# Attention by FFT products: two of four product sums made by accumulating DMAs, the constant's row put in ahead of them, correlation tiles handled in pairs

## What is computed

```python
qf = jnp.fft.fft(q, axis=2)
kf = jnp.fft.fft(k, axis=2)
corr = jnp.fft.ifft(qf * jnp.conj(kf), axis=2).real
topk = int(C * np.log(L))                       # 12
w, idx = jax.lax.top_k(corr.transpose(0, 1, 3, 2), topk)
w = jax.nn.softmax(w, axis=-1)
...
for i in range(topk):
    g = jnp.minimum(idx[:, :, None, :, i] + pos, L - 1)
    out = out + w[:, :, None, :, i] * jnp.take_along_axis(v, g, axis=2)
...
x = x + _L0_xattn_ref(_layernorm(x, axis=-1), ctx_4096, ctx_4096)
x = x + _L0_ffn_ref(_layernorm(x, axis=-1), A_w, B_w, Wq_w, keys)
```

## Time and profile before

| | |
|---|---|
| median of 3 runs | 2241.87 us (2239.7 to 2241.94) |
| profiled execution: span | 2240.4 us |
| PE, DVE, POOL, ACT busy | 97%, 76%, 70%, 55% of the span |
| a normal step, from one L578 to the next | 41.53 us |
| a normalizer step | 42.64 us |
| steps 3 to 30 | 22 normal, 6 normalizer |

### The profile page before, as it was taken

One profiled execution on the slowest core, in us unless ns is written; L12 is line 12 of the kernel. 1 busy time (PEld: TensorE's weight loads), 2 busy tenths in 40 slices (PEclk: granted clock), 3 DMA queues, 4 the chain that ended last, 5 costly groups with the idle time before them and its releaser, 6 DMA issues.

```text
span 2240.4 us, 30428 instructions
## 1 busy us (share of the span) xinstructions
PE 2170.8 (97%) x9664; PEld 1460.5 (65%) x9664; DVE 1712.2 (76%) x4081; ACT 1222.0 (55%) x2486; POOL 1570.1 (70%) x1023
## 2 busy tenths in 40 slices
PE   4899999999999999999999998899999999999999
PEld 2466565565565565565565564687888888787887
DVE  7999999999999999999999999744544444454443
ACT  4576676676676676676655535544434334443431
POOL 6899999999999999999999987433333333333420
PEclk9999999999999999999999999999999999999999
DMA  8132332332332332332321245544444444444431
GB/s 288 65 120 99 111 110 99 116 106 99 118 104 99 118 104 99 118 103 99 103 82 61 91 164 176 186 157 164 151 162 166 167 160 161 157 159 161 164 116 57
DMA packets 110420, 287.84 MB, mean 128 GB/s; under 512 B 7136, under 2 KB 7264, under 8 KB 109152
## 3 DMA queue, kind: packets, MB, share of 16 engines
q1 hardware_dynamic: 110304, 286.45, 37.1%
HBM read 219.32 MB, written 67.11 MB: 128 GB/s over the span
## 4 chain that ended last, share of the span: by engine, by line
PE 77%; DVE 11%; POOL 5%; issue 4%; ACT 2%; DMA 1%; SPq 0%; DVEq 0%; POOLq 0%; ACTq 0%
PE pair L691 7%; PE out L528 5%; PE out L530 5%; PE out L529 5%; PE z L528 5%; PE z L530 5%; PE z L529 5%; PE evac L602 4%; PE evac L603 4%; PE pair L528 4%; PE evac L578 4%; PE pair L530 4%; PE pair L529 4%; PE lag L642 4%; PE pair L591 4%
## 5 line engine op out<-in xcount | busy, mean ns | idle before, releaser
L1549 POOL TENSOR_TENSOR rows<-rows,cin 128x1024 f32<-128x1024 f32 x48 | 117.9, 2456 | 355.8 <-DMA rows<-out_dram 292.8
L691 PE MATMUL pair<-r_f,back 128*128 128x512 f32 x768 | 335.4, 593 | 0.0
L1495 POOL TENSOR_TENSOR r_f<-prod 128x1024 f32<-128x1024 f32 x128 | 306.0, 2402 | 24.0 <-DVE prod L931 22.1
L691 PEld LDWEIGHTS pair<-r_f,back 128*128 128x128 f32 x768 | 143.3, 190 | 167.8 <-issue 167.8
L528 PE MATMUL pair<-w_hi,wts_hi 128*128 128x512 f32 x512 | 206.5, 403 | 4.9 <-DVE w_lo L1049 2.9
L1244 ACT ACTIVATE xt_full<-tp 128x512 f32<-128x512 f32 x128 | 74.8, 584 | 245.4 <-PE tp L547 242.0
L528 PE MATMUL out<-b_hi,zt_hi 128*128 128x512 f32 x512 | 205.8, 402 | 1.5 <-ACT zt_hi L1433 1.5
L528 PE MATMUL z<-a_hi,xt 128*128 128x512 f32 x512 | 203.0, 397 | 1.9 <-DVE xt L888 1.9
L530 PE MATMUL pair<-w_hi,wts_lo 128*128 128x512 f32 x512 | 200.5, 392 | 0.0
L529 PE MATMUL pair<-w_lo,wts_hi 128*128 128x512 f32 x512 | 200.4, 391 | 0.0
L529 PE MATMUL z<-a_lo,xt 128*128 128x512 f32 x512 | 200.1, 391 | 0.0
(11 more groups left out here) (193 smaller groups left out, 5619.2 us busy)
## 6 DMA issues: line engine op xcount, KB each, us to landing
out_dram<-att_sb SPq DMA_DIRECT2D x32, 1024.0 KB, 4.3
rows<-out_dram SPq DMA_DIRECT2D x64, 512.0 KB, 3.6
cin<-out_dram SPq DMA_DIRECT2D x64, 512.0 KB, 4.0
xin<-in_x_dram SPq DMA_DIRECT2D x64, 512.0 KB, 3.7
out_dram<-rows SPq DMA_DIRECT2D x64, 512.0 KB, 2.6
vf<-in_ctx_dram SPq DMA_DIRECT2D x31, 1024.0 KB, 5.2
xf<-in_x_dram SPq DMA_DIRECT2D x30, 1024.0 KB, 5.1
stat_in<-in_x_dram SPq DMA_DIRECT2D x28, 1024.0 KB, 5.1
```

The costliest lines, as they stand in the source:

```text
L691: return nc.tensor.matmul(pair_ps[:, bank, :], back[:, 3 * bank + n, :], r_f[:, row, :], start=n == 0, stop=n == 2)
L1495: nc.gpsimd.tensor_tensor(dst, prod[:, slot, 0:2, :], prod[:, slot, 2:4, :], ALU.add).then_inc(add_done, 1)
L1549: nc.gpsimd.tensor_tensor(half, first, second, op).then_inc(c_added, 1)
```

## The change

**Product sums.** DVE writes the first product of a block straight into its place in `r_f` (or `p_f`) and the second into `prod`, which now has four slots of two rows. For x and for n = 0, 1 POOL adds `prod` to that place, still one TENSOR_TENSOR each. For n = 2, 3 POOL issues a DMA that adds `prod` to `r_f` where it lies (`send_products`, semaphores `cyc_summed` and `odd_summed`). One of POOL's four instructions that fold ctx now stands between the two DMAs.

**The constant.** ACT writes the row right after DVE's first product of n = 2 (`first_put`), ahead of the DMA, and in ACT's order between `row_sums` and `row_squares`.

**The statistics' load** (`stat_in`, on SP) also waits until the second DMA has landed.

**Pairs.** `lag_ps` is one tensor of two banks. ACT's L1297 and L1300 and DVE's L961, L964, L972 and L975 become one instruction for two tiles each. So do the negation of the maximum, a memset and the reciprocal in the top 12.

```diff
-                def sums_of(tiles):
...
-                    for second in (0, 1):
-                        for t in tiles:
...
-                                dve.wait_ge(cos_copied, CT * i + t + 1)
-                                op = nc.vector.tensor_tensor(cos_ps, cos_in, sin_ps, ALU.add)
...
+                def sums_of(pair):
+
+                    t = pair[0]
+                    both = slice(t, t + 2)
+                    cos_in = e[:, both, 0:2 * P].rearrange("p t (s n) -> p t s n", n=P)[:, :, :, 1:]
...
+                    dve.wait_ge(cos_copied, pair_at(i, t))
+                    nc.vector.tensor_tensor(cos_ps, cos_in, sin_ps, ALU.add).then_inc(lag_folded, 1)
+                    dve.wait_ge(lag_folded, corr_at(i, t, 0))
+                    nc.vector.tensor_tensor(sin_ps, cos_in, sin_ps, ALU.subtract).then_inc(lag_folded, 1)
...
+                    dve.wait_ge(low_copied, pair_at(i, t))
+                    nc.vector.tensor_tensor(total, high, low, ALU.add).then_inc(corr_summed, 1)
+                    dve.wait_ge(corr_summed, corr_at(i, t, 0))
+                    nc.vector.tensor_tensor(low, high, low, ALU.subtract).then_inc(corr_summed, 1)
...
+                def lag_copies(pair):
+                    t = pair[0]
+                    both = slice(t, t + 2)
+                    act.wait_ge(lag_ready, CT * i + t + 2)
+                    nc.scalar.activation(e[:, both, 0:2 * P], lag_ps[:, :, 0:2 * P], ACT.Copy).then_inc(cos_copied, 1)
+                    act.wait_ge(lag_folded, corr_at(i, t, 1))
...
             def add_products(idx, slot, dst):
                 pool.wait_ge(prod_ready, idx + 1)
-                nc.gpsimd.tensor_tensor(dst, prod[:, slot, 0:2, :], prod[:, slot, 2:4, :], ALU.add).then_inc(add_done, 1)
+                nc.gpsimd.tensor_tensor(dst, dst, prod[:, slot, :, :], ALU.add).then_inc(add_done, 1)
+
+            def send_products(i, n, signal):
+                blk = W_BLOCKS[n]
+                pool.wait_ge(prod_ready, prod_w(i, n) + 1)
+                nc.gpsimd.dma_start(r_f[:, 2 * blk:2 * blk + 2, :], prod[:, n, :, :], accum_op=ALU.add).then_inc(signal, 16)
...
+                def put_constant():
+                    act.wait_ge(first_put, 2 * i - 1)
+                    act.wait_ge(dc_ready, i)
+                    nc.scalar.activation(r_f[0:1, 0, :], v_cyc[before][0:1, 0, :], ACT.Copy).then_inc(dc_put, 1)
...
-                    pe.wait_ge(add_done, prod_w(i, 2) + 1)
-                    pe.wait_ge(dc_put, i)
+                    pe.wait_ge(cyc_summed, 16 * i)
                     out_row(0, 2)
                     out_row(1, 2).then_inc(pair_ready, 1)
...
-                    pe.wait_ge(add_done, prod_w(i, 3) + 1)
+                    pe.wait_ge(odd_summed, 16 * i)
                     out_row(2, 2)
                     out_row(3, 2).then_inc(pair_ready, 1)
...
                         sp.wait_ge(stat_used, LT * (g + 1))
+                        if b:
+                            sp.wait_ge(odd_summed, 16 * i)
                         load_stat(g // GPB - 1, g % GPB, stat_in[:], stat_loaded)
```

More of the change, by code:

```diff
@@ L188, in build_program @@
         evac_ps = [ps(f"evac{s}", [P, CH]) for s in range(2)]
-        lag_ps = [ps(f"lag{s}", [P, L]) for s in range(2)]
+        lag_ps = ps("lag", [P, 2, L])
         pair_ps = ps("pair", [P, 4, CH])
@@ L641, in lag_share @@
                     cols = (slice(0, P), slice(3 * P + 1, L), slice(P, 2 * P), slice(2 * P, 3 * P + 1))[row]
-                    return nc.tensor.matmul(lag_ps[t % 2][:, cols], p_f[:, row, t * P:(t + 1) * P], lags[:, cols],
+                    return nc.tensor.matmul(lag_ps[:, t % 2, cols], p_f[:, row, t * P:(t + 1) * P], lags[:, cols],
                                             start=True, stop=True)
@@ L919, in body, with products @@
                 cur, before = (r + 1) % 2, r % 2
-                def products(idx, pair, vs, plus_one):
+                def products(first, pair, second, vs, plus_one):
                     c_ps, s_ps = (pair_ps[:, 2 * pair + part, :].unsqueeze(1).broadcast_to((P, 2, CH)) for part in range(2))
-                    slot = prod[:, pair, :, :]
-                    if not (isinstance(idx, int) and idx < 2):
-                        dve.wait_ge(add_done, idx - 1)
                     if plus_one:
-                        nc.vector.scalar_tensor_tensor(slot[:, 0:2, :], c_ps, 1.0, vs[:, 0:2, :], ALU.add, ALU.mult)
+                        nc.vector.scalar_tensor_tensor(first, c_ps, 1.0, vs[:, 0:2, :], ALU.add, ALU.mult).then_inc(first_put, 1)
                     else:
-                        nc.vector.tensor_tensor(slot[:, 0:2, :], c_ps, vs[:, 0:2, :], ALU.mult)
-                    nc.vector.tensor_tensor(slot[:, 2:4, :], s_ps, vs[:, 1:3, :], ALU.mult).then_inc(prod_ready, 1)
+                        nc.vector.tensor_tensor(first, c_ps, vs[:, 0:2, :], ALU.mult)
+                    nc.vector.tensor_tensor(second, s_ps, vs[:, 1:3, :], ALU.mult).then_inc(prod_ready, 1)
                 def evac_sin(n, i=i, cur=cur):
@@ L992, in topk @@
                     elif stage == 4:
-                        dve.wait_ge(topk_step, topk_at(i, t, 3))
-                        op = nc.vector.memset(top[:, t, TOPK:16], NEG)
+                        dve.wait_ge(topk_step, topk_at(i, t + 1, 3))
+                        op = nc.vector.memset(top[:, t:t + 2, TOPK:16], NEG)
                     else:
@@ L1010, in topk_stages @@
                     for stage in stages:
-                        for t in pair:
+                        for t in pair[:1] if stage in (1, 4) else pair:
                             topk(t, stage)
@@ L1029, in body @@
                         dve.wait_ge(minus_done, 4 * i + n + 1)
-                        products(prod_x(i, n), n, v_cyc[cur][:, 3 * n:3 * n + 3, :], False)
+                        if not is_step(i, 0):
+                            dve.wait_ge(lag_ready, CT * i)
+                            dve.wait_ge(add_done, (add_x(0, n) if is_step(i, 1) else add_w(i - 1, n)) + 1)
+                        products(p_f[:, 2 * n:2 * n + 2, :], n, prod[:, n, :, :], v_cyc[cur][:, 3 * n:3 * n + 3, :], False)
                         if n == 0 and not (is_step(i, 0) or is_step(i, 1)):
@@ L1065, in body @@
                         vs = (v_cyc if blk < 2 else v_neg)[before][:, 3 * (blk % 2):3 * (blk % 2) + 3, :]
-                        products(prod_w(i, n), n % 2, vs, blk < 2)
+                        if n == 0 and not is_step(i, 1):
+                            dve.wait_ge(pair_ready, pair_out(i - 1, 1) + 1)
+                        if n < 2:
+                            dve.wait_ge(add_done, (add_x(i, n) if a else add_w(i - 1, n)) + 1)
+                        products(r_f[:, 2 * blk:2 * blk + 2, :], n % 2, prod[:, n, :, :], vs, blk < 2)
                         if n == 0 and s and r == 3:
@@ L1366, in body @@
                     row_sums(i + 2)
+                    put_constant()
                     row_squares(i + 2)
+                elif b and i + 1 < GROUPS:
+                    put_constant()
                 if i + 2 < GROUPS and r == 3:
@@ L1382, in body @@
                     part_high(3)
-                if b:
-                    act.wait_ge(add_done, prod_w(i, 2) + 1)
-                    act.wait_ge(dc_ready, i)
-                    nc.scalar.activation(r_f[0:1, 0, :], v_cyc[before][0:1, 0, :], ACT.Copy).then_inc(dc_put, 1)
+                if b and i + 1 >= GROUPS:
+                    put_constant()
                 if a:
@@ L1585, in body @@
                 if a:
-                    if not is_step(i, 0):
-                        pool.wait_ge(lag_ready, CT * i)
                     for n in range(2):
@@ L1603, in body @@
                 if b:
-                    if not is_step(i, 1):
-                        pool.wait_ge(pair_ready, pair_out(i - 1, 1) + 1)
-                    for n in range(4):
+                    for n in range(2):
                         blk = W_BLOCKS[n]
-                        add_products(prod_w(i, n), n % 2, r_f[:, 2 * blk:2 * blk + 2, :])
+                        add_products(prod_w(i, n), n, r_f[:, 2 * blk:2 * blk + 2, :])
                         if n == 0 and s and r == 3:
@@ L1611, in body @@
                             normalizers(k + 2)
+                    pool.wait_ge(dc_put, i)
+                    send_products(i, 2, cyc_summed)
+                if f and not is_step(i, 0):
+                    middle_fold_v(i + 1)
+                if b:
+                    send_products(i, 3, odd_summed)
                 if is_step(i, GROUPS - 1):
```

82 lines of the change are left out of this document (37 added, 45 removed).

## The result

The changed kernel takes 2479.74 us (median), the kernel before beside it 2241.66: a ratio of 1.1061, 95% interval 1.1043 to 1.1079. One of four executions of the changed kernel took 4401.4 us, for a reason that no run shows; the other three lie between 2477.4 and 2480.69, and the ratio goes by them. The forecast was 2289, with a range of 2264 to 2316. The sign was right; the loss is 238 us where 47 were forecast.

A forecast was written before the change was run, and what follows sets the result against it. PE, DVE and POOL each nearly bound a step, with PE waiting twice for DVE's chain through `sums_of`; 22 x 1.61 + 6 x 1.06 + 5.5 = 47.3 us more gave 2289 us, range 2264 to 2316.

The forecast's parts named there:

- The joined negation and memset: DVE's top 12: they wait for the second tile's MAX8, which ends when they would have been done anyway; cost nothing.
- Joined sums: DVE and ACT chains over tile pairs: 1.05 us plus 0.56 us, so a normal step is 1.61 us longer.
- Smaller loss: Rival: ACT, busy only 27.39 us of a step, could catch up, so the 0.56 us is absorbed; 2271 us, chance 0.16.
- pair 2, 3: Joined chain of tiles 2 and 3: 3.50 us against 2.87, cost 0.63, or 0.56 after a reciprocal's saving.
- DMAs late: Rival: accumulating DMAs take 8.0 us to land, PE waits 0.8 us in `out_row` in 32 steps; 2315 us, chance 0.18.
- the rest, 5.5 us: Steps 0 to 2 and 31, same chains without some meetings: 5.5 us for the four, between 2 and 7.
- Normalizer steps: POOL's relief gives back 0.95 of 1.61 us, ACT's new order costs 0.4: 1.06 us longer in each of six.
- Constant and `stat_in`'s load at nothing: ACT's earlier constant in a normal step and SP's later load of the statistics: both forecast to cost nothing.
- Faster: Rival: half as many DVE instructions cost less, no lateness at PE's block n = 2; 2236 us, chance 0.12.
- no change: Rival: losses and POOL's relief cancel, needing the first pair's cost alone below 0.3 us; chance 0.04.
- meeting 1: PE's block n = 2 starts right behind DVE's second product of n = 0, without slack; forecast to move 1.05 us.
- main case: Whole kernel: the forecast's own sum, 2289 us, own range 2280 to 2298, chance 0.50.

The follow-up runs named there:

- experiment 1: Changed kernel with the negation of the maxima again one single-column DVE instruction per tile: 2301.73 us, ratio 1.0271.
- experiment 2: Kernel before the change with only the negation of two tiles' maxima joined into one DVE instruction: 2281.9 us, ratio 1.0185.
- experiment 8: Changed kernel with the joined negation as zeros minus top, a tensor-tensor with two sources in SBUF: 2479.23 us.
- experiment 7: Changed kernel with the joined negation as a reduction over one element with the sign turned: 2298.61 us.
- experiment 4: Changed kernel with single negations and with sums and copies by tile again; DMAs, constant, later load, joined memset and reciprocal stay: 2245.18 us, ratio 1.0018.
- experiment 3: Changed kernel with the joined negation over three columns instead of two, the third a spare: 2478.08 us.
- experiment 6: Changed kernel, joined negation left in, with the two accumulating DMAs replaced by POOL additions: 2332.37 us.
- experiment 9: Changed kernel with one more wait on POOL, between the two last folds of v: 2404.23 us.
- experiment 10: Changed kernel with single negations and only tiles 2 and 3 joined in sums and copies, tiles 0 and 1 by tile: 2275.85 us, ratio 1.0157.
- experiment 5: Changed kernel with single negations and the two accumulating DMAs replaced by POOL additions: 2296.04 us, ratio 1.0246.

## Why the prediction was wrong

**The step that failed** is the sentence "The joined negation and memset wait for the second tile's MAX8, which ends when they would have been done anyway: nothing." It priced the negation by when its inputs are ready, and took for granted that an instruction over 128x2 numbers lasts about what one over 128x1 does. Experiments 1 and 2 show it from both sides: taken out of the change it gives back 178 us, put into the kernel before it costs 41. Per step it is 0.65 + 5.40 = 6.05 us for two joined negations against 2 x 0.21 for four single ones (746.08 to 746.29 for two): 5.6 us. The step shrinks by 49.2 - 43.4 = 5.8, so practically all of it lies on the path, for ACT's exponentials and DVE's own next stages stand behind it. The other 0.2 us the runs do not tell apart; the lower clock below is one candidate.

**The mechanism**, as far as it is shown: a tensor-scalar over more than one column between places in SBUF, the memory that holds the tensors, that comes while a POOL instruction is under way waits for its end (0.65 and 5.40 us); so does a tensor-tensor with two sources in SBUF (0.65 and 5.41 us, experiment 8); a tensor-scalar over one column and a reduction over two don't (0.15 us each, experiments 1 and 7). Nor does the joined reciprocal, 128x2 as well: 0.15 to 0.17 us in experiment 4, where 33 of its 64 lie within a POOL instruction. An even count isn't needed (5.43 us over three columns, experiment 3). The Trainium skill (SBUF — State Buffer, Who interferes with whom) has a rule for this: VectorE and GpSimd share a second pair of SBUF ports, whoever comes first keeps it for a whole instruction, and of the operations here tensor_scalar can want it, a tensor_tensor with two inputs in SBUF wants it against a GpSimd instruction that reads SBUF, and tensor_reduce never does. The joined negations (5.40 us) and experiments 8 (5.41 us) and 7 (0.15 us) agree with the three. That it is kept for one whole instruction agrees with experiments 2 and 6 (1.12 and 0.90 us, one POOL instruction each) and not with the changed kernel, where the wait went through two. By that rule the joined negation was the edit to suspect.

From rows alone a rival was missing too: a wait of up to one POOL fold, 2.33 us, twice a step.

**Why 5.4 and not 2.4.** In experiments 2 and 6 the negation waited for one POOL instruction. In the changed kernel it comes while POOL is at the second DMA issue (685.36, issue 684.86 to 686.06), and then both folds run, with no wait between them; with a wait between them it gets in after the first (experiment 9). So the length is that of the folds, and not of the DMA. The DMA brings the meeting about, as far as the order on POOL tells: its issue stands where an addition of 2.4 us was. Whether folds that follow without a wait keep the ports, or POOL had taken both up while the issue was still running (its rows overlap by 0.67 us there and by 0.04 elsewhere), stays open. Against the first speaks that folds of `pick` also follow each other without a wait, and behind the one at 651.82 the negation did get in, as it did in experiment 2 between an addition and a fold.

**Point by point.**

- *Joined sums (1.61 a normal step with the reciprocal).* Measured by experiments 1 and 4: 1.74, and 0.16 for the rest of the edits. Chain 3.42 us (3.38 forecast); in experiment 1 it starts 0.67 us after PE's last lag record, as forecast (the kernel before: 0.01). The mechanism was right, the size 0.3 too small.
- *The 0.16 us.* Negation and memset now start behind the second MAX8, where the kernel before had those of the first tile run beside it. The timelines bear this out: from a pair's first MAX8 to the next MATCH_VALUE_LOAD it is 1.47 us in experiment 4 and 1.41 before, twice a step; in the next round of tiles 0 and 1, where the memset stands in that place, it is 1.58 against 1.46. That is 0.24 us more, less 0.07 for each of the two joined reciprocals. It was not tried alone.
- *Smaller loss* (0.56 absorbed) fell: experiment 10 shows pair 2, 3 on the path, with 0.93 us, of which about 0.58 without the raise by 2.
- *DMAs late* fell in the steady steps (4.8 us to landing; 1216.8 against 1216.9 in experiment 5). At the end it held: waits of 3.4 and 3.8 us in the last two steps (experiment 4), 5.7 us of the time (experiment 5), where the cover is gone. That is most of what "the rest, 5.5 us" was short: tail and start lost 11.6 us in experiment 1.
- *Normalizer steps.* 0.95 forecast as given back: experiment 4 shows 42.62 becoming 41.81, 0.81 less though a normal step lost 0.16, so the relief is 0.97, the size forecast. The 0.4 for ACT's order did not come (43.57 with joined sums, 43.41 in a normal step). But the relief was not the DMAs' doing where the sums are joined: in experiment 5, with POOL additions, a normalizer step takes 43.60 us. The longer step alone gives POOL the time that it lacked, so beside joined sums the DMAs gave nothing back.
- *Constant and `stat_in`'s load at nothing.* Nothing of them shows in experiment 4's steps.
- *Faster* and *no change* need meeting 1 to stay; it moved (PE waits 1.02 us there).

Without the negation the forecast's sum would have been 47 us against 59 between the profiled spans of experiment 1 and the kernel before (2301.7 us: within the full range, above the main case's own 2280 to 2298). Of the 12 missing, 6 lie in the 28 steps (47.8 where 41.8 were forecast) and 6 in the tail and the start (11.6 where 5.5 were).

**The clock** adds a little. In every step of the kernel after PE idles twice, for 2.0 us at its start and for 2.0 to 3.4 us soon after, and the granted clock is below 1 in each: 0.97 over the step from 646.68, and 0.90 over that from 794.22, one of every fourth. There PE idles 2.02 and 2.63 us, and the windows show half the clock behind it (the row's last but two is the granted clock, 0.50 being the lower level of 1.2 GHz):

```profile
794.22:798.00 3.78, 2.69 (x4) 0.65 (x4) 3.05 (x5) 1.94 (x5) 0.69 (x2) 0.64 0.01 2
798.00:802.00 4.00, 2.46 (x3) 1.17 (x4) 3.92 (x14) 3.18 (x6) 4.00 (x7) 0.50 0.01 4
```

The seven steps of this kind take 50.4 us instead of 49.2: 9 us in all. They come with PE's idling and left with it: in experiment 1, where PE idles 0.4 to 1.0 us at a time, the clock is 1.00 in each of the 28 steps (over the span 0.992, against 0.961). What the lower clock costs in the other steps is not told apart.

## What to carry to other kernels

Before two small VectorE instructions become one, ask whether the joined form needs what GpSimd holds. In these runs a tensor-scalar over several columns in SBUF, or a second source in SBUF, waited out whole GpSimd instructions, and the wait showed as the instruction's own duration. A reduction over one element did the same work in 0.15 us. Joining tiles in a chain of dependent instructions trades covered latency for open latency; price it by the chain's ends, not by the instructions saved. A DMA that is hidden in every steady step can still be open in the last one.

## What the runs showed that was not expected

- A 128x2 instruction of VectorE took 0.29 to 5.45 us; its end followed a GpSimd instruction's by 0.02 to 0.04 us.
- It can wait through two GpSimd instructions in a row (5.40 us), and a semaphore wait put between those cut it to 3.12 us and the kernel by 75 us.
- GpSimd's folds around its DMA issue are recorded at 2.7 to 3.0 us instead of 2.4, with the issue itself at 0.9 to 1.2 us; from 684.86 to 690.73 is 5.87 us, room for an issue of 1.2 and two folds of 2.35, so the spans rather than the work seem longer.
- Raising a semaphore by 2 instead of 1 made the waiting instruction start 0.10 to 0.11 us after the end instead of 0.03 to 0.04, 18.7 us over the kernel (one execution).
